# Two alternating buffers instead of one for the SiLU result of the quantised FFN stage

## The reference, cut to what matters

```python
def fp4_quant_dequant(x):                      # blocks of 16 along the last dimension
    xb = x.reshape(shape[:-1] + (shape[-1] // 16, 16))
    scale = jnp.maximum(jnp.max(jnp.abs(xb), axis=-1, keepdims=True) / 6.0, 1e-12)
    idx = jnp.searchsorted(_MID, jnp.abs(xb / scale))
    return (_GRID[idx] * jnp.sign(xb / scale) * scale).reshape(shape)

def fp4_linear(x, w):
    return jnp.einsum('bsk,nk->bsn', fp4_quant_dequant(x), fp4_quant_dequant(w))

def _L0_ffn_ref(x, w_gate, w_up, w_down):      # x (4, 4096, 1024), inner width 2816
    gate = fp4_linear(x, w_gate)
    y = fp4_linear(x, w_up)
    h = jax.nn.silu(gate) * y
    return fp4_linear(h, w_down)

xn = _layernorm(x)
return x + attn(xn) + _L0_ffn_ref(xn, w_gate, w_up, w_down)
```

## Time and profile before

| | |
|---|---|
| median of 3 runs | 3741.72 us (3737.19 to 3785.76) |
| profiled execution | 3727.35 us |
| its span, slowest core (core 3) | 3725.7 us |
| spans of the 8 cores | 3707.4 to 3725.7 us |
| mean granted TensorE clock, cores | 0.850 to 0.854 |
| busy over the span: PE, DVE, ACT | 69%, 66%, 33% |
| fifth block | about 2701 us to the end |

### The profile page before, as it was taken

One profiled execution on the slowest core, in us unless ns is written; L12 is line 12 of the kernel. 1 busy time (PEld: TensorE's weight loads), 2 busy tenths in 40 slices (PEclk: granted clock), 3 DMA queues, 4 the chain that ended last, 5 costly groups with the idle time before them and its releaser, 6 DMA issues. The chain is left out here.

```text
span 3725.7 us, 35974 instructions; the slowest of 8 cores (3707.4 to 3725.7 us)
## 1 busy us (share of the span) xinstructions
PE 2556.8 (69%) x9848; PEld 953.9 (26%) x9848; DVE 2448.1 (66%) x3881; ACT 1244.2 (33%) x1963; POOL 106.1 (3%) x199
## 2 busy tenths in 40 slices
PE   1111396389797988979798897947955664656666
PEld 1111242022222222222222222212423232223332
DVE  8888802449677694958768593963158678188585
ACT  1111231155555555555555555510012122022121
POOL 0000000000000000000000000000000000000000
PEclk9999997589797998979798897966967786877877
DMA  1111230001010010101101010153330100900302
GB/s 35 34 34 34 91 47 0 7 14 43 24 37 31 30 39 21 41 24 38 33 27 40 20 40 17 39 89 77 136 88 0 62 29 7 177 1 0 91 0 79
DMA packets 126527, 156.27 MB, mean 42 GB/s; under 512 B 77824, under 2 KB 88320, under 8 KB 124288
## 3 DMA queue, kind: packets, MB, share of 16 engines
q1 hardware_dynamic: 41056, 110.25, 9.6%
q10 hardware_dynamic: 69312, 17.31, 3.4%
q0 software_dynamic: 15968, 26.42, 2.9%
HBM read 98.89 MB, written 46.66 MB: 39 GB/s over the span
## 5 line engine op out<-in xcount | busy, mean ns | idle before, releaser
L762 ACT ACTIVATE pbuf<-psA,negB_col 128x512 bf16<-128x512 f32 x512 | 352.0, 688 | 347.4 <-PE psA L748 347.4
L762 ACT ACTIVATE pbuf<-psB,negB_col 128x512 bf16<-128x512 f32 x512 | 351.4, 686 | 284.9 <-PE psB L748 284.0
L778 PE MATMUL psD<-pbuf,V_h 128*128 128x512 bf16 x1024 | 304.4, 379 | 27.5 <-ACT pbuf L762 27.5
L778 PE MATMUL psC<-pbuf,V_h 128*128 128x512 bf16 x1024 | 308.7, 383 | 18.0 <-ACT pbuf L762 18.0
L748 PE MATMUL psA<-qT_all,kT_h 128*128 128x512 bf16 x1024 | 314.5, 389 | 0.4 <-DVEq L720 0.4
L748 PE MATMUL psB<-qT_all,kT_h 128*128 128x512 bf16 x1024 | 313.7, 388 | 0.0
L211 DVE TENSOR_REDUCE pbm<-wbuf 128x32 f32<-128x512 f32 (+1 forms) x136 | 90.3, 664 | 231.3 <-DMA WgqN<-wqout 86.4
L1014 PE MATMUL psC<-hqT_b,wdq_b 128*128 128x512 bf16 x704 | 168.3, 403 | 42.8 <-DVE obuf L1027 39.5
L778 PE MATMUL psE<-pbuf,V_h 128*1 128x512 bf16 x512 | 194.5, 380 | 0.0
L778 PE MATMUL psF<-pbuf,V_h 128*1 128x512 bf16 x512 | 193.0, 377 | 0.0
L341 PE MATMUL psA<-ident_t,xq_f 128*128 128x128 f32 x64 | 17.4, 428 | 241.0 <-DVE xq_f L253 241.0
(11 more groups left out here) (199 smaller groups left out, 4630.6 us busy)
## 6 DMA issues: line engine op xcount, KB each, us to landing
xbuf<-x_tok SPq DMA_DIRECT2D x16, 1024.0 KB, 5.3
rbuf<-resid_scr SPq DMA_DIRECT2D x32, 512.0 KB, 7.0
wbuf<-Wg SPq DMA_DIRECT2D x44, 256.0 KB, 2.8
wbuf<-Wu SPq DMA_DIRECT2D x44, 256.0 KB, 2.7
wbuf<-Wd SPq DMA_DIRECT2D x40, 256.0 KB, 2.7
xt_buf<-xT_own SPq DMA_DIRECT2D x8, 1024.0 KB, 6.9
resid_scr<-rstage SPq DMA_DIRECT2D x8, 1024.0 KB, 4.7
resid_scr<-obuf SPq DMA_DIRECT2D x16, 512.0 KB, 6.0
```

Source lines behind the costliest of these rows:

```text
L762: eb.em('scalar', lambda e, cglob=cglob, pb=pb: e.activation(out=pbuf[:, cglob % 2, :], in_=pb[:, :], func=AF.Exp, bias=negB_col[:], scale ...
L778: ins = (lambda e, kc=kc, cg=cg, lo=lo, hi=hi, dstp=dstp, dsl=dsl: e.matmul(dstp[dsl, 0:512], V_h[:, kc, lo:hi], pbuf[:, cg % 2, :], start ...
```

## The change

`gs_c` gets a second half of 2 KB in each partition. The chunks use the halves in turn, by the number of products emitted so far. ScalarE's Silu of a chunk waits for the product of the chunk before the last one, no longer for that of the last one: that is the product which read the half it writes. Nothing else in the waits, the order of instructions on any engine, or the work is changed. The buffers allocated behind `gs_c` (`h_t`, `hq_t`, `hqT_b`, `rbuf`, `obuf`) lie 2 KB further on in each partition.

```diff
-    gs_c = sb("gs_c", [128, 512], F32, es_b5)
+    gs_c = sb("gs_c", [128, 2, 512], F32, es_b5)
@@
+                    gb = S['hbld'].n % 2
                     eb.wait('scalar', S['ffh'], S['ffh'].n)
-                    if S['hbld'].n > 0:
-                        eb.wait('scalar', S['hbld'], S['hbld'].n)
+                    if S['hbld'].n > 1:
+                        eb.wait('scalar', S['hbld'], S['hbld'].n - 1)
                     S['sil'].n += 1
-                    eb.em('scalar', lambda e, clen=clen, pg=pg: e.activation(
-                        out=gs_c[:, 0:clen], in_=pg[:, 0:clen], func=AF.Silu).then_inc(S['sil'].h, 1))
+                    eb.em('scalar', lambda e, clen=clen, pg=pg, gb=gb: e.activation(
+                        out=gs_c[:, gb, 0:clen], in_=pg[:, 0:clen], func=AF.Silu).then_inc(S['sil'].h, 1))
                     eb.wait('vector', S['sil'], S['sil'].n)
                     S['hbld'].n += 1
-                    eb.em('vector', lambda e, c0=c0, clen=clen, py=py: e.tensor_tensor(
-                        out=h_t[:, c0:c0 + clen], in0=gs_c[:, 0:clen], in1=py[:, 0:clen],
+                    eb.em('vector', lambda e, c0=c0, clen=clen, py=py, gb=gb: e.tensor_tensor(
+                        out=h_t[:, c0:c0 + clen], in0=gs_c[:, gb, 0:clen], in1=py[:, 0:clen],
                         op=ALU.mult).then_inc(S['hbld'].h, 1))
```

## The result

| | before | after |
|---|---|---|
| median | 3735.12 us (8 runs) | 3693.10 us (8 runs) |
| ratio | 1 | 0.9889, 95% interval 0.9877 to 0.9901 |
| span of the profiled execution, slowest core | 3725.7 us (core 3) | 3692.2 us (core 0) |
| spans of the 8 cores | 3707.4 to 3725.7 | 3674.9 to 3692.2 |
| fifth block, mean of the 8 cores | 1017.2 us | 974.9 us |

The prediction was 3700 us against a median of 3741.72, a ratio of 0.9889. With more runs of both kernels the median of before came down by 6.6 us, and the measured ratio is 0.9889 too.

A forecast was written before the change was run, and what follows sets the result against it. The prediction took the fifth block to be bound by a chain between engines, with VectorE's waits for the Silu on the path. 28 tiles x 1.48 us = 41.4 us off the median of 3741.72 gave 3700 us, range 3682 to 3722.

The forecast's parts named there:

- What bounds the block: Fifth block: no engine is full; a chain between engines binds, with VectorE waiting 139.6 us for ScalarE's Silu.
- The wait of c1 and of c2: At a tile boundary, VectorE's gaps of 0.79 and 0.69 us: the product of chunk c2 starts 1.48 us earlier.
- What lies behind it: After the product of c2: copies and absolute value move along by 1.48 us; the 0.79 us before L227 stay.
- margin of 0.55 us: At a tile boundary, TensorE's transposes are in time for ScalarE's third copy with 0.55 us to spare.
- The number of tiles: Of the block's 32 tiles, 28 gain; in 4 the chunks come too late from TensorE.
- The overlap at no cost: ScalarE's Silu of c1 running beside VectorE's quantisation was costed at 0.
- The sum: Over the fifth block: 28 x 1.48 = 41.4 us less, giving a median of 3700 us.
- offset of 14.4 us: The median of the runs shown, 3741.72 us, lies 14.4 us above the profiled execution of 3727.35.
- The clock: TensorE's idle stretch before the transposes shortens by 1.48 us, yet its clock stays down there.
- the clock stays up: Rival, 10%: transposes at full clock bring L227 another 0.30 us sooner per tile, 50 us in all, 3692 us.

The follow-up runs named there:

- half-step: Two kernels: the changed kernel with only the Silu wait of chunk c1 relaxed, or only that of c2; ratios to before 0.9949 and 0.9950.
- waitmove: The changed kernel with ScalarE's wait for the product of c2 moved behind the three copies of the tile before; ratio to before 0.9842.
- one late matmul: The changed kernel with 1 unused 512-column matmul (0.43 us) ahead of each tile's transposes; no ratio, product of c2 to L227 stays 4.25 us.
- three: The changed kernel with 3 unused 512-column matmuls (1.28 us) ahead of each tile's transposes; ratio to before 0.9951.
- 30 matmuls: The changed kernel with 30 unused matmuls in TensorE's idle stretch before most tiles' transposes; no ratio, stretches of tiles 438.3 and 450.7 us.

## Why the prediction was right

- *What bounds the block.* Confirmed. The gain is the fall of VectorE's waits for the Silu (41.9 us), and the 404.6 us of the longest wait in the earlier trace rows were the wrong row to count.
- *The wait of c1 and of c2.* Confirmed. 1.48 us worked out, 2.85 - 1.37 = 1.48 us measured, and each half-step within 0.01 us (0.88 for 0.87, 0.77 for 0.77).
- *What lies behind it.* The wait before L227 stayed at 0.79 us. The margin of 0.55 us was checked from three sides: `waitmove` gains 0.55, one late matmul is free, three cost 0.66 of 1.28, which leaves 0.62.
- *The number of tiles.* 28, by the count of waits. The c2 of tile 0 of half 1 waits for TensorE as before.
- *The overlap at no cost.* The products take 0.68, 0.68 and 0.56 us against 0.68, 0.69 and 0.56, and the quantisation 1.62 to 1.63 as before.
- *The sum.* 41.4 us for 42.3 us of the block, partly by luck, as said at the result. Of the offset of 14.4 us between the profiled execution and the median, 6.6 us were the sample of three runs.
- *The clock: outcome right, one step wrong.* The prediction says that the change shortens TensorE's idle stretch before the transposes by 1.48 us. It does not. These lines of after answer to the earlier trace rows:

```profile
3058.15 1.09 PE L977 MATMUL psB<-ident_t,hq_t 128*128 128x128 f32 x4 [8.26 <-DVE hq_t L253]
...
3060.61 0.87 PE L977 MATMUL psB<-ident_t,hq_t 128*128 128x128 f32 x3 [0.52 <-ACT hqT_b L988]
```

The idle stretch is 8.26 us here (8.09 before). Over the ordinary boundaries of the 8 cores its mean is 8.15 us, where it was 7.42: it grew. The 1.48 us came out of the gap between the second and the third group of transposes, 2.00 us before and 0.52 now. The reason was in the prediction's own rows: the chunks follow the third group, which follows the copies, which follow the product of c2; the next transposes follow the quantisation, which follows the same product. Both ends of the long idle stretch hang on it and move together. What shrinks is the distance between two things of which only one hangs on it: the first two groups hang on the quantisation of the tile before, the third on the product. The 0.73 us of growth mean that TensorE got through the third group and the chunks sooner; its mean granted clock rose from 0.850 to 0.854 before to 0.858 to 0.861, and nothing on the path waited for it. The rival built on that step (the clock stays up, 10%) had its price about right, 0.30 us for 0.35, but the change could not bring it about by the step that it named. The Trainium skill (TensorE: Matmul & The Clock Gate, "HAM oscillation — how this bites in real kernels") says that closing idle gaps keeps the clock up. The trace with 30 matmuls agrees in the main: the first group kept the full clock in 103 of the 104 tiles in which at most 2.0 us were left, and the third in 71 of them; the 29 tiles with the least idle time are the exception, as said above.

## What to carry to other kernels

A single buffer between two engines costs a wait for each use, here 0.79 and 0.69 us, but only where both engines could otherwise run on. Count out the uses at which a third engine delivers too late, here 4 of 32 tiles, and read the gain from the idle time of the engine that is on the path, not from the longest wait in the list. Before a gain is passed on down the chain, look up what else the next instruction waits for, and compute how much earlier that is ready; here it was 0.55 us, and it bounded the next edit too. Where a stretch of idle time seems to shrink, check whether its two ends don't hang on the same event. And where an experiment is to fill idle time, look tile by tile at what is left of it before reading the outcome.

## What the runs showed beside this

The weight loads between the groups differ much between the cores. On ScalarE's queue the 27 transposing DMAs took 93.3 us on core 0 of after:

```profile
3149.33 36.36 ACTq L1122 DMA_TRANSPOSE wgq_b<-WgqN  x8
3185.72 40.40 ACTq L1126 DMA_TRANSPOSE wuq_b<-WuqN  x8
3226.21 16.43 ACTq L1043 DMA_TRANSPOSE wdq_b<-WdqN  x11
```

They took 82.4 to 89.8 us on the seven others, and 77.4 to 95.6 us on the cores of before. The stretches of tiles on either side differ by at most 4.8 us between the cores of one kernel, but the cores also start the block up to 11.8 us apart. In after core 0 is the slowest and has the longest loads; in before the longest are on core 1, 0.2 us behind the slowest. So the loads and the start together choose the slowest core. No run here shows why one core draws longer loads than another.
